# A fused two-layer attention kernel: x's transposes moved from between the turns of P to between P times V and V

## The reference

```
# layer 0: 16 heads of 64
x = attn(ln(x), ln(x)) + x            # SELF:  q, k, v from ln(x); softmax(q k^T / 8) v, then Wo
x = attn(ln(x), context) + x          # CROSS: k and v from the context
x = geglu(ln(x)) + x                  # GEGLU
# layer 1: 16 heads of 8
out = attn(x, context)                # CROSS2
out = out + ffn(ln(out))              # FFN
return x + out
```

## Time and profile before

| | us |
|---|---|
| median of three runs | 451.22 |
| the profiled execution's own time | 450.97 |
| its span, first to last instruction | 449.3 |
| TensorE matmuls busy | 434.4 (97%) |
| TensorE weight loads busy | 399.4 (89%) |
| VectorE busy | 352.9 (79%) |
| ScalarE busy | 318.8 (71%) |
| GpSimd busy | 201.8 (45%) |

### The profile page before, as it was taken

The page is one execution under the profiler, slowest core; times in us unless marked ns, Lnnn a source line. Parts: engine busy times, 40 slices in busy tenths (PEclk is TensorE's granted clock), DMA queues, the critical chain, the costliest instruction groups (busy, mean ns, idle before and its releaser), DMA issues.

```text
span 449.3 us, 17107 instructions
## 1 busy us (share of the span) xinstructions
PE 434.4 (97%) x7513; PEld 399.4 (89%) x7513; DVE 352.9 (79%) x649; ACT 318.8 (71%) x587; POOL 201.8 (45%) x226
## 2 busy tenths in 40 slices
PE   8999999999999999999999999999999999999897
PEld 7979999898999999989989899889999777778797
DVE  4888889688797887978978789896784788898471
ACT  5686676777778768787677776876546576777763
POOL 1883332555345634555352533523342232152782
PEclk9999999999999999999999999999999999999999
DMA  7202021110200000000000000000000000000011
GB/s 230 58 4 85 3 85 28 53 48 4 63 4 4 10 3 11 12 3 10 12 2 12 3 10 13 3 3 1 2 1 19 10 12 19 4 1 4 13 36 47
DMA packets 14623, 10.61 MB, mean 24 GB/s; under 512 B 5188, under 2 KB 13592, under 8 KB 14552
## 3 DMA queue, kind: packets, MB, share of 16 engines
q1 hardware_dynamic: 14120, 9.48, 7.3%
q10 hardware_dynamic: 432, 0.07, 0.1%
HBM read 8.50 MB, written 1.05 MB: 21 GB/s over the span
## 4 chain that ended last, share of the span: by engine, by line
PE 88%; DVE 6%; ACT 2%; issue 2%; POOL 1%; DMA 1%; POOLq 0%
PE stage L683 12%; PE stage L684 11%; PE stage L685 11%; PE scp L865 8%; PE scp L788 7%; PE scp L837 6%; PE scp L944 6%; PE out0p L885 4%; PE out0p L913 4%; PE out0p L887 3%; PE out0p L886 3%; PE stage L849 3%; PE scp L805 2%; DVE pr L1417 1%; PE stage L934 1%
## 5 line engine op out<-in xcount | busy, mean ns | idle before, releaser
L1734 POOL TENSOR_TENSOR pr<-pr,rc 128x1024 f32<-128x1024 f32 (+1 forms) x32 | 59.1, 1867 | 76.5 <-DVE rc L1447 76.4
L1165 ACT ACTIVATE pr<-pr 128x1024 f32<-128x1024 f32 x48 | 50.8, 1059 | 36.7 <-DVE pr L1417 30.1
L1672 POOL TENSOR_TENSOR rstd<-veps,neghalf 128x2 f32<-128x2 f32 x32 | 22.8, 714 | 70.8 <-DVE veps L1365 70.6
L1099 ACT ACTIVATE vt<-stage 64x512 f32<-64x512 f32 x83 | 49.2, 592 | 4.8 <-PE stage L685 1.2
L1461 DVE COPY vt<-stage 64x512 f32<-64x512 f32 x45 | 31.2, 694 | 21.8 <-PE stage L685 20.9
L1412 DVE TENSOR_REDUCE mx<-scp 128x16 f32<-128x1024 f32 x32 | 39.2, 1224 | 8.9 <-PE scp L788 8.5
L1099 ACT ACTIVATE ot_h<-scp 128x512 fp32r<-128x512 f32 x64 | 33.4, 600 | 13.3 <-PE scp L865 13.3
L1467 DVE TENSOR_TENSOR ot_r<-scp,ot_h 128x512 fp32r<-128x512 f32 x64 | 40.0, 683 | 2.3 <-ACT ot_h L1099 1.0
L1099 ACT ACTIVATE k_of_heads<-stage 128x512 f32<-128x512 f32 x62 | 36.9, 598 | 5.4
L1417 DVE TENSOR_TENSOR pr<-scp,mx 128x1024 f32<-128x1024 f32 x32 | 39.2, 1224 | 1.1
L1445 DVE TENSOR_REDUCE sm<-pr 128x16 f32<-128x1024 f32 x32 | 38.0, 1188 | 0.0
(11 more groups left out here) (266 smaller groups left out, 1398.8 us busy)
## 6 DMA issues: line engine op xcount, KB each, us to landing
ctx_in<-in_ctx_dram SPq DMA_DIRECT2D x16, 96.0 KB, 2.0
masked_k<-in_L_xattn_Wo_dram SPq DMA_DIRECT2D x2, 512.0 KB, 3.8
out_dram<-rows SPq DMA_DIRECT2D x8, 128.0 KB, 1.8
rows<-in_x_dram SPq DMA_DIRECT2D x1, 768.0 KB, 9.4
pr<-in_L_xattn_Wq_dram SPq DMA_DIRECT2D x1, 512.0 KB, 4.9
pr<-in_L_xattn_Wk_dram SPq DMA_DIRECT2D x1, 512.0 KB, 6.2
pt<-in_L_xattn_Wv_dram SPq DMA_DIRECT2D x1, 512.0 KB, 7.6
rows<-in_L_xattn_Wq_dram SPq DMA_DIRECT2D x1, 512.0 KB, 5.1
```

The costliest lines, as they stand in the source:

```text
L1099: return nc.scalar.activation(dst, s, ACT.Copy)
L1165: nc.scalar.activation(pr[t][:, :], pr[t][:, :], ACT.Exp, scale=scale[s.phase]).then_inc(exped, 1)
L1734: nc.gpsimd.tensor_tensor(p, p, rc[:, t, h:, None].to_broadcast([ROWS, H - h, N]), ALU.mult)\
```

## The change

On TensorE and on ScalarE the step for x of group `two` goes from between the two turns of P to behind P times V and ahead of V. `Counts` follows. VectorE's and GpSimd's lists are as they were, and GpSimd keeps both multiplies of each group.

```
@@ Counts.group, SELF and CROSS @@
             else:
-                self.x(two.phase, two.first)
                 for i in range(4):
                     self.use("av", p, g, i)
+                self.x(two.phase, two.first)
                 self.vals(one.phase, one.first, range(3))
@@ TensorE, group @@
                     turn_step(s, 0)
                     if before:
                         out_turn_step(before)
-                    x_step(two, s)
                     turn_step(s, 1)
                     av_step(s, 0)
                     av_step(s, 1)
+                    x_step(two, s)
                     val_step(one, range(3), s)
@@ ScalarE, group @@
                 if s.phase in (SELF, CROSS):
                     pt_step(s, 0)
-                    x_turned_step(two)
                     pt_step(s, 1)
                     av_step(s, 0)
                     av_step(s, 1)
+                    x_turned_step(two)
                     val_step(one, range(3))
                     x_high_step(two)
```

## The result

The changed kernel takes 457.91 us (median of four runs, 456.84 to 459.58) against 451.05 us for the kernel before beside it: ratio 1.0155, 95% interval 1.0127 to 1.0182. It is slower by 6.9 us. The forecast was 455.2 with a range up to 457.4: the sign and the places were right, and the size lies outside the range. The profiled execution took 458.37 us, its span 456.6, so 7.3 more than before's 449.3.

A forecast was written before the change was run, and what follows sets the result against it. TensorE, 97% busy, was taken as the bound, with GpSimd's second multiply releasing turn 1. Six groups at 0.22, the vectors' group 0.28 and eight at 0.33 sum to 4.24 us: 455.2 us, range 452.8 to 457.4.

The forecast's parts named there:

- The hold by GpSimd: Turn 1 of P on TensorE waits for GpSimd's second multiply, so it begins no sooner than 12.86 us after scores.
- the gain of 0.15 with context: CROSS groups: without x ahead of turn 1, P times V begins 13.89 instead of 14.04 us after scores.
- x's own price: x's transposes, uncovered between P times V and V, lengthen the way to scores by 0.22, with context 0.43 us.
- The failed step: V's third step waits for ScalarE's copy of x, queued behind four ot_h copies: level in SELF, 0.05 us late with context.
- rival B: x's copy becomes the next wait at V's third step: 0.15 us more in 14 groups, 457.3 us; chance 0.20.
- the vectors' group: The group that also turns the vectors: x costs 0.53, P times V gains 0.25, so 0.28 us.
- upper bound of 7.4: Sum with x in full everywhere, 5.3 us, and 0.15 for each of 14 late x copies.
- rival C: TensorE's three "issue" pauses, about 2.1 us, go into the new waits: 453.1 us; chance 0.10.
- rule of occupancy: Limiting engine found by busy share: GpSimd at 45% limits nothing, TensorE's work is unchanged, sum 0 (451.0 us).

The follow-up runs named there:

- The two half multiplies: GpSimd's multiply for row tile 1 over 8 of 16 heads only, in the changed kernel (455.74 us) and in the kernel before (450.59 us).
- the memset: Kernel before plus one GpSimd memset of a spare tile between its two multiplies in 15 groups: 451.71 us, ratio 1.0020.
- the shifted pair: Kernel before and changed kernel, each with 64 redundant waits ahead of TensorE's first instruction: 453.93 and 460.76 us.

## Why the prediction missed by its size

**The hold by GpSimd: right.** 12.81 us from scores to pair end, and 13.89 from scores to P times V, came out to 0.02 us in every undisturbed group, the gain of 0.15 with context included. The exceptions are SELF 0 and CROSS 6, where P times V waits for the pt copies as before (14.42 and 14.37). The two half multiplies and the memset show that GpSimd releases turn 1 in either kernel; before, x was hidden behind it.

**x's own price: right, a little high.** 0.22 and 0.43 forecast, 0.20 and 0.40 measured.

**The failed step is ScalarE's: a restart that I put at nothing.** I wrote that V's third step "takes x's stage bank, three uses on, and so waits for that copy", and found it "level" in SELF and 0.05 late with context. It costs 0.17 and 0.21. The copy is where I put it: in SELF it starts 68.95 - 65.81 = 3.14 after P times V. The slip is in how a wait works on TensorE. I compared the hand-over with the start of V's third *matmul*. But the wait holds its *weight load*, which before was 0.23 us ahead of the matmul (68.23 and 68.46) and after a wait begins with it (69.59 and 69.59), so a copy that comes level with the matmul is a wait already. And behind that wait the step to the scores takes 70.48 - 69.59 = 0.89 instead of 69.23 - 68.46 = 0.77. These 0.12 us are the missing term. The rest is small: the hand-over comes 0.64 after the copy's start and not 0.61, and x takes 0.02 to 0.03 less, so V's third step would have come sooner. In SELF that is -0.01 + 0.12 + 0.03 + 0.02 = 0.16, and with context 0.05 + 0.12 + 0.01 + 0.03 = 0.21.

Not all of the load's wait is paid for, since the load had a lead. SELF 3 of the changed kernel shows it with a shorter wait. These are V's first matmul, the weight load of its third step, and the scores:

```profile
87.90 0.48 PE L683 MATMUL stage<-wv_of0h,src0h 128*128 128x512 f32 x1
...
89.32 0.19 PEld L683 LDWEIGHTS stage<-wv_of0h,src0h 128*128 128x128 f32 x1 [0.22 <-ACT xT L1118]
...
90.22 1.84 PE L788 MATMUL scp<-k_of_heads,q_of_heads 64*64 64x64 f32 x107
```

The load comes 1.42 after V's start there, and 87.64 - 86.37 = 1.27 in the kernel before. It is 0.15 late, and the scores only 0.05 (2.32 after V's start instead of 2.27). In SELF 2 it is 0.28 late and costs 0.17, in CROSS 2 it is 0.32 late (222.03 - 220.44 against 216.64 - 215.37) and costs 0.21. In all three 0.10 or 0.11 of the delay is free, which is the lead of 0.23 less the restart of 0.12.

With 0.12 in each of 14 groups the forecast would have been 4.2 + 1.7 = 5.9. That is rival B in all but its cause: B had 0.15 more in each, from a slower hand-over or a later ScalarE, of which only 0.03 and 0.01 came true. My two causes do not exclude each other, and I gave them chances as if they did.

From the two groups subtracted above the correction is 6 times (0.17 - 0.02) + 8 times (0.21 - 0.05 - 0.03), which is 1.9, so 4.2 becomes 6.1 where 5.7 was measured. Most of the difference lies in two groups: CROSS 3 has no such wait (0.2 less), and the vectors' group came out cheaper than its 0.28 (18.65 against 18.44 in the shifted pair, where it holds no pause: 0.21).

**The failed step alone would not have missed the range.** Steady time is 1.5 us over the sum (5.7 against 4.2), and the pauses add 1.6, a term that the forecast held at no change. With either one alone the time would have been 456.7 to 456.8, inside the range up to 457.4. The sum had an upper bound of 7.4, which holds what was measured, but the range stopped at B.

**The pauses went the other way than rival C.** C let 2.1 us of them vanish into the new waits. They grew by 1.6, and by 1.5 in the second trace of the changed kernel. With 5.7 that makes the 7.3 of the two spans. In the ratio of the timed runs they cannot be told apart from the rest.

**What stays open.** In the traces the pauses of SELF and CROSS stand only at fixed counts of TensorE's instructions, 3009, 4033, 8897 before and 3009, 3265, 4033, 8898, 9154 after: all 193 or 194 beyond a multiple of 256, and so are those of the shifted pair, to 2. (A pause of 0.91 us behind CROSS, in every kernel, is of another kind: it stays with its work when the counts are shifted.) A transfer of 16 KB on the queue for instructions follows each such count, mostly within 2 us and sometimes after 4 to 8; the page has 58 of them, 0.95 MB. Most counts of this kind have no pause. The stretch of the changed kernel behind the pause at 87.27 shows it, the queue's line first in a window from 86 to 93 us (packets, MB, share of 16 engines):

```profile
q8 instruction: 1, 0.02, 0.8%
```

The same window of the kernel before has two:

```profile
q8 instruction: 2, 0.03, 1.9%
```

The first of before's two comes 1.6 us after its pause, the one after the change 3.1 us after it, and there the next count of 256 pauses as well (92.81). That looks like code that arrives late, but I have no run that makes the transfers earlier or later by themselves, so why a changed order lengthens them is not shown. The Trainium skill, Advanced Engine Details and Errata, ISA Cache, says that the instructions of an engine are held in blocks of 16 KB, 256 instructions each; by that rule the trace agrees in size and in spacing, and the page gives no price for a late one.

The Trainium skill's rule of occupancy (Perfetto Trace Analysis, Identifying the Most-Contended Engine) would have given no change. The trace disagrees: GpSimd is 44% busy and holds 15 turns of P.

## What to carry to other kernels

Before work is taken out of a stretch, subtract that stretch end to end. If another engine's chain from the last dependence to the release has a fixed length (12.81 us here), what stands in it is free, as long as what reads its result isn't held up by its place (x ahead of turn 0 cost nothing, x behind the scores 11 us), and costs its full time outside. When a margin at a wait is worked out for TensorE, compare with the start of the weight load to see whether there is a wait. For its price take how late the matmul comes and add the restart, here 0.12 us; a copy that comes level with the matmul is not free. And check rivals for whether they can be true together: then they are terms, not cases.

## What the runs showed of the hardware that I had not expected

- TensorE's weight load of V's 128x512 steps runs 0.23 us ahead of its matmul. A wait loses this lead, and the step behind starts 0.12 us later than in the flow (0.89 against 0.77 after the matmul). Of the delay of the load 0.10 or 0.11 us was free, whether it was 0.15, 0.28 or 0.32.
- Pauses of 0.3 to 1.5 us at instruction counts that are multiples of 256 apart, at the same places in both traces of the changed kernel, with other lengths. 32 more event instructions ahead moved them to other work. With a reordering that left every steady period as it was they came to 3.8 instead of 2.1 us.
- GpSimd's hand-over to a weight load took 0.05 us at every load that waited for it, in all twelve traces, whether SELF or CROSS. A memset recorded with 0.20 us delayed what followed by 0.15.
